# The last steps of a fused attention and feed-forward kernel: alternating PSUM banks, a resting GpSimd, and a last batch stored in halves

## The reference

```python
x = x + attn_a(layernorm(x))   # 16 heads of 64; softmax(q) over features, softmax(k) over tokens,
                               # context = q^T k per head (64x64), then out @ w_out + b_out
x = x + ffn(layernorm(x))      # k_act = relu(xk @ W_k)^2; sigmoid(xr @ W_r) * (k_act @ W_v)
x = x + attn_b(layernorm(x))   # 16 heads of 8 with rotary q and k, full 512x512 softmax, then W_O
x = x + ffn(layernorm(x))      # the same weights again
```

## The kernel before, in words

| step | a | s | l | b | e | us from the span's start |
|---|---|---|---|---|---|---|
| 16 (paired, no A) | - | 15 | 14 | 13 | 12 | about 832 to 885 |
| 17 (draining) | - | - | 15 | 14 | 13 | 885 to 934 |
| 18 (draining) | - | - | - | 15 | 14 | 934 to 972 |
| 19 (draining) | - | - | - | - | 15 | 972 to the end |

## Time and profile before

### The profile page before, as it was taken

How to read it: one execution, slowest core, us unless ns; L and a number is a source line. 1 busy time by engine, 2 the same in 40 slices (tenths; PEclk the granted TensorE clock), 3 DMA queues, 4 the chain that set the end, 5 groups by cost and what they waited for, 6 DMA issues and landing times.

```text
span 1002.2 us, 24337 instructions
## 1 busy us (share of the span) xinstructions
PE 915.6 (91%) x9807; PEld 532.2 (53%) x9807; DVE 651.2 (65%) x1542; ACT 674.6 (67%) x671; POOL 505.9 (50%) x346
## 2 busy tenths in 40 slices
PE   4987989999999999999999999999999998797973
PEld 3775545555555555555555555555555555332322
DVE  4777656668586777668586777668586565635233
ACT  4465677777777777777777777777777777665860
POOL 3758284645566475545566475545566464405000
PEclk9999999999999999999999999999999999998995
DMA  5013243233241423233241423233232323123210
GB/s 165 23 33 103 60 126 90 90 98 115 62 132 52 137 66 98 94 98 115 61 130 54 137 66 101 91 96 116 61 118 57 127 67 121 50 72 99 71 31 16
DMA packets 68669, 87.64 MB, mean 87 GB/s; under 512 B 13633, under 2 KB 40130, under 8 KB 68546
## 3 DMA queue, kind: packets, MB, share of 16 engines
q1 hardware_dynamic: 68546, 85.96, 28.4%
HBM read 16.19 MB, written 20.97 MB: 37 GB/s over the span
## 4 chain that ended last, share of the span: by engine, by line
PE 64%; DVE 14%; ACT 13%; issue 5%; SPq 2%; POOL 1%; DMA 1%; ACTq 0%; DVEq 0%
PE PS L1607 17%; PE PS L1563 9%; PE PS L1407 8%; ACT work L704 6%; PE PS L1409 5%; PE PS L1408 5%; PE PS L1475 5%; PE PS L1521 4%; ACT work_b L704 3%; DVE cT L1099 3%; PE PS L1515 3%; DVE cT L1101 3%; PE PS L1402 2%; PE PS L1504 2%; PE PS L1580 1%
## 5 line engine op out<-in xcount | busy, mean ns | idle before, releaser
L704 ACT ACTIVATE work<-PS 128x2048 f32<-128x2048 f32 x150 | 281.6, 1877 | 53.7 <-PE PS L1563 53.7
L694 ACT ACTIVATE work<-PS 128x512 f32<-128x512 f32 x256 | 152.5, 599 | 175.3 <-PE PS L1409 173.5
L454 POOL TENSOR_TENSOR rs<-ve,half_neg 128x4 f32<-128x4 f32 x64 | 64.8, 1012 | 335.7 <-DVE ve L919 335.7
L1607 PE MATMUL PS<-work,v 128*32 128x512 f32 x1368 | 175.1, 604 | 0.5 <-ACT work L711 0.5
L467 POOL TENSOR_TENSOR work<-work,q_rcp 128x1024 f32<-128x1024 f32 x64 | 122.3, 1911 | 96.4 <-DVE q_rcp L971 59.0
L704 ACT ACTIVATE work_b<-PS 128x2048 f32<-128x2048 f32 x74 | 138.9, 1877 | 24.1 <-PE PS L1563 23.9
L1407 PE MATMUL PS<-wqk,h1h 128*128 128x512 f32 x256 | 124.9, 488 | 5.7 <-issue 2.6
L1563 PE MATMUL PS<-q_st,k_st 32*128 32x512 f32 x896 | 113.8, 496 | 17.6 <-ACT work L704 7.8
L1409 PE MATMUL PS<-wqk,h1l 128*128 128x512 f32 x256 | 101.5, 396 | 0.0
L1408 PE MATMUL PS<-wqk,h1h 128*128 128x512 f32 x256 | 101.2, 395 | 0.0
L1029 DVE SCALAR_TENSOR_TENSOR gated<-gate,PS 128x512 f32<-128x512 f32 x32 | 22.0, 688 | 110.5 <-PE PS L1528 110.5
(11 more groups left out here) (166 smaller groups left out, 1670.6 us busy)
## 6 DMA issues: line engine op xcount, KB each, us to landing
qkv_scratch<-qkv_sb SPq DMA_DIRECT2D x16, 768.0 KB, 4.6
rot<-qkv_sb SPq DMA_DIRECT2D x32, 256.0 KB, 2.4
k_st<-qk_hi SPq DMA_DIRECT2D x128, 64.0 KB, 2.1
q_st<-qk_hi SPq DMA_DIRECT2D x128, 64.0 KB, 2.1
k_st<-qk_lo SPq DMA_DIRECT2D x128, 64.0 KB, 2.1
q_st<-qk_lo SPq DMA_DIRECT2D x128, 64.0 KB, 2.1
parted<-U SPq DMA_DIRECT2D x52, 128.0 KB, 2.9
xa<-in_attn_a_x SPq DMA_DIRECT2D x16, 256.0 KB, 3.3
```

What stands on the lines that cost most here:

```text
L454: pool.tensor_tensor(rs[:, :], ve[:, :], half_neg[:, :], ALU.pow).then_inc(rstd[n].sem, 1)
L694: act.activation((EQ, EK)[r // 2][c % 2][:, (r % 2) * 512:(r % 2) * 512 + 512], PS[:, bank, :], ACT.Exp)\
L704: act.activation(probs_of(z, b, n), PS[:, 0:4, :], ACT.Exp).then_inc(z["s_exp"].sem, 1)
L1607: mm = pe.matmul(PS[32 * h:32 * h + 32, 6, :], v_flat[p][:, kc, at:at + 32], probs_of(z, b, n)[:, h, :], start=(n % 8 == 0), stop=(n % 8 = ...
```

## The change

Steps 0 to 15 are the same instruction for instruction. In step 16, which has no attention A, the products alternate between banks 7 and 4; in the draining steps POOL waits until DVE has finished the layer norm with index 3 (`rest_for_norm`) before it starts on the rotary embedding, and DVE does that norm before `pv_copy`; `mixed_k` is scaled and mixed before `mixed_r` is begun; for the last batch DVE does the square too, `ffn_r` goes to bank 5 and doesn't wait for `relu`, the value product is written to two banks in halves, and the output leaves in two DMAs. `judge_sums` is moved behind the last output. The core of the diff (what is left out are the definitions of three semaphores, the choice of `other`, which is bank 7 with A and 4 without, and the passing of it through `t_copy`, `relu`, `gate_v` and `p_copy`):

```diff
 # SP, draining_step
-                store_out(z, ffn[1], e)
+                if there(b):
+                    store_out(z, ffn[1], e)
+                else:
+                    for half in range(2):
+                        cs = slice(2 * half, 2 * half + 2)
+                        hold(sp, last_x, 0, 2 * half + 2)
+                        sp.dma_start(out_view[e][:, cs, :], out_sb[:, cs, :])\
+                          .then_inc((last_out, z["out_st"])[half].sem, 16)
 # POOL, draining_step
                 rsqrt_var(3, e)
+                rest_for_norm(3, e)
                 if there(l):
...
-                hold(pool, f2["v"], e - 1)
-                square(f2, e)
+                if there(i - 3):
+                    hold(pool, f2["v"], e - 1)
+                    square(f2, e)
 # ACT, paired_step: p_copy(l, 1) only with A; DVE, paired_step, after p_copy(l, 0)
+                    if not A:
+                        p_copy(l, 1, other)
 # ACT, draining_step
-                        gates(f2, e)
+                        gates(f2, e, 4 if there(b) else 5)
 # DVE
+            def mix_k_first(f, j):
+                hold(dve, f["hT"], j)
+                for n in (1, 0):
+                    dve.tensor_scalar(f["mixed"][n][:, :], PS[:, 7, :], mu[:, n:n + 1], None, ALU.mult)\
+                       .then_inc(f["mu"].sem, 1)
+                    hold(dve, f["mu"], j, 2 - n)
+                    dve.scalar_tensor_tensor(f["mixed"][n][:, 1:N], PS[:, 7, 0:N - 1], mu[:, 2 + n:3 + n],
+                                             f["mixed"][n][:, 1:N], ALU.mult, ALU.add).then_inc(f["mix"].sem, 1)
+            def end_half(f, j, half):
+                cs = slice(2 * half, 2 * half + 2)
+                hold(dve, f["gate"], j)
+                hold(dve, last_v, 0, half + 1)
+                dve.scalar_tensor_tensor(gated[:, cs, :], f["gate_sb"][:, cs, :], 1.0, as_chunks(PS[:, (7, 4)[half], :])[:, cs, :],
+                                         ALU.add, ALU.mult).then_inc(last_x.sem, 1)
+                hold(dve, last_x, 0, 2 * half + 1)
+                dve.scalar_tensor_tensor(out_sb[:, cs, :], gated[:, cs, :], 0.5, x3[:, cs, :], ALU.mult, ALU.add)\
+                   .then_inc(last_x.sem, 1)
 # DVE, draining_step
                 x3_stats(z, 3, e)
+                ln_norm(3, e, x3, hn2)
                 if B:
                     pv_copy(z, b, 0)
-                ln_norm(3, e, x3, hn2)
-                scale_and_mix(f2, e)
+                mix_k_first(f2, e)
                 hold(dve, ffn[0]["act"], NB - 1)
-                relu(f2, e)
-                if at_batch(i, NB + 3):
+                if B:
+                    relu(f2, e)
+                else:
+                    relu_sq(f2, e)
+                if B:
+                    gate_v(f2, e) ... add_gated, normalise as before
+                else:
+                    hold(dve, z["out_st"], e - 1)
+                    for half in range(2):
+                        end_half(f2, e, half)
                     judge_sums()
 # PE, paired_step
+                banks, other = ((7,), 7) if A else ((7, 4), 4)
                     if k == 0 and E:
-                        proj_b(l, 1)
+                        if not A:
+                            hold(pe, ph_exp, s)
+                        proj_b(l, 1, banks)
                     if k == 1:
-                        hold(pe, p_ev, l, 3 if E else 1)
-                        ctx_wout(s, spacer=False)
+                        hold(pe, p_ev, l, 1 if not E else 3 if A else 2)
+                        ctx_wout(s, (5, other), spacer=False)
                     if k == 4:
-                        hold(pe, f1["mix"], s)
-                        ffn_k(f1, s, 7)
+                        if A:
+                            hold(pe, f1["mix"], s)
+                        else:
+                            hold(pe, t_ev, s)
+                        ffn_k(f1, s, other)
                     if k == 5:
                         hold(pe, f1["gate"], s)
-                        ffn_v(f1, s)
+                        ffn_v(f1, s, other)
                     if k == 5 and E:
-                        hold(pe, f1["x"], s, 1)
+                        if A:
+                            hold(pe, f1["x"], s, 1)
                         ffn_T(f2, 3, e)
 ... k == 6 and k == 7: ffn_k and ffn_v of f2 to bank `other` in the same way
                     if k == 7:
-                        if E:
+                        if E and A:
                             hold(pe, f2["x"], e, 1)
+                        elif E:
+                            hold(pe, f2["gate"], e)
                         h3_transposes(s)
 # PE, draining_step
                     if n == 12:
-                        ffn_r(f2, e)
+                        if B:
+                            ffn_r(f2, e)
+                        else:
+                            hold(pe, z["x3_ok"], e)
+                            ffn_r(f2, e, "k", 5)
                     if n == 2:
-                        hold(pe, ph_exp, NB - 1)
+                        hold(pe, f2["x"], e - 1, 1)
                     if n == 14:
-                        ffn_v(f2, e)
+                        if B:
+                            ffn_v(f2, e)
+                        else:
+                            last_ffn_v(f2, e)   # chunks 0, 1 to bank 7, then 2, 3 to bank 4, a signal after each pair
```

More of the change, by code:

```diff
@@ L435, in _ @@
                 iterations(filling_step, paired_step, draining_step)
+                hold(sp, last_out, 0)
                 hold(sp, att[0]["out_st"], NB - 1)
@@ L827, in paired_step @@
                 z, f1, f2 = att[0], ffn[0], ffn[1]
+                other = 7 if A else 4
                 for k in range(8):
                     exp_scores(z, b, 2 * k)
-                    if E and k == 1:
+                    if A and E and k == 1:
                         hold(act, qkv_st, l - 1)
@@ L836, in paired_step @@
                     if k == 2:
-                        t_copy(s)
+                        t_copy(s, (5, other))
                     if not E and k == 3:
@@ L1244, in paired_step @@
                 hold(dve, f2["act"], e - 1)
-                relu(f1, s, 7)
+                relu(f1, s, other)
                 if A:
                     sums_of(a, 2)
-                gate_v(f1, s)
+                gate_v(f1, s, other)
                 if E:
@@ L1253, in paired_step @@
                     hold(dve, f1["act"], s)
-                    relu(f2, e, 7)
+                    relu(f2, e, other)
                 ln_norm(2, s, x2, h3)
@@ L1258, in paired_step @@
                 if E:
-                    gate_v(f2, e)
+                    gate_v(f2, e, other)
                     hold(dve, z["out_st"], e - 1)
@@ L1530, in ffn_v, with last_ffn_v @@
                 mm.then_inc(f["v"].sem, 1)
+            def last_ffn_v(f, j):
+                hold(pe, f["act"], j)
+                for c in range(NC):
+                    mm = pe.matmul(PS[:, (7, 4)[c // 2], c * D:(c + 1) * D], f["k_act"][:, c * P:(c + 1) * P], WvfT,
+                                   start=True, stop=True)
+                    if c % 2 == 1:
+                        mm.then_inc(last_v.sem, 1)
             def h3_transposes(j):
@@ L1761, in paired_step @@
                     if k == 4:
-                        hold(pe, f1["mix"], s)
-                        ffn_k(f1, s, 7)
+                        if A:
[3 more added lines that the diff above has]
+                        ffn_k(f1, s, other)
                     if k == 5:
                         hold(pe, f1["gate"], s)
-                        ffn_v(f1, s)
+                        ffn_v(f1, s, other)
                     if k == 6 and E:
-                        hold(pe, f2["mix"], e)
-                        ffn_k(f2, e, 7)
+                        if A:
+                            hold(pe, f2["mix"], e)
+                        else:
+                            hold(pe, f1["x"], s, 1)
+                        ffn_k(f2, e, other)
                     if k == 7 and E:
                         hold(pe, f2["gate"], e)
-                        ffn_v(f2, e)
+                        ffn_v(f2, e, other)
                     if A:
@@ L1855, in draining_step @@
                         hold(pe, f2["mix"], e)
-                        ffn_v(f2, e)
+                        if B:
+                            ffn_v(f2, e)
+                        else:
+                            last_ffn_v(f2, e)
                     if n == 15 and B:
```

18 lines of the change are left out of this document (9 added, 9 removed).

## The result

| | before | after |
|---|---|---|
| median | 1005.38 us (1004.83 to 1007.34, 4 runs) | 994.49 us (992.9 to 995.64, 4 runs) |
| ratio to before, 95% interval | | 0.9887 [0.9869, 0.9905] |
| profiled execution: own time, span | 1004.03, 1002.2 us | 995.63, 993.8 us |

The median is 2.8 us above the forecast of 991.7 and inside its range. A second set of six runs gave 994.44 us (0.9898 [0.9877, 0.9919]). The profiled executions differ by 8.40 us only, because that of before lay 1.35 us under its median and that of after 1.14 us above.

What follows compares the result with a forecast made beforehand. PE bounds the kernel, with its gaps in the last steps. Terms 2.46 + 0.75 + 7.93 - 0.30 + 0.74 + 2.12 + 0.40 = 14.10 us off 1004.03 give 989.93, plus 1.80 for the median: 991.7, range 988.9 to 997.0.

Steps and rivals of the forecast that it cites:

- the norm beside POOL: Step 17: DVE's layer norm no longer waits for POOL; 6.09 us of PE wait plus 1.84 of slow clock, 7.93.
- the stacks before step 18: Batch 15's stack DMAs, now held by POOL, land late for step 18's first tile: 0.30 us lost, bounds 0 and 3.
- the 1 us that the prediction named as a sign of being wrong: The prediction counts as wrong if step 18 starts with a wait over 1 us.
- rival (a): The stacks replace the norm as the wait: PE idles 3 us, the clock drops, time 996.2; chance 0.09.
- Step 18: The norm runs before pv_copy, so PE's wait goes: 0.74 us gained, bounds 0.5 and 0.74.
- step 19: The serial last feed-forward shortens by 2.12 us; 0.45 more if the full clock returns before ffn_v.
- Rival (b): Step 16 is held by the exps and DVE, so the free bank buys nothing: time 994.9; chance 0.07.
- (c): Step 17's norm is slow for a reason other than POOL and still takes 6.45 us: time 996.6; chance 0.02.
- (d): Slower than before: DVE's steady work in step 17 shuts POOL out and stretches the rotary chain; chance 0.03.
- The clock in step 16: A shorter gap and denser PE work may keep the clock full: 0.75 us gained, bounds 0 and 1.25.
- The cover of M: Step 16: DVE ready for M at 849.7, PE at 849.8; if this fails, some tenths are lost.
- the 0.40: Program end: the last DMA, halved to 128 KB, finishes 0.40 us sooner, bounds 0 and 1.4.

Runs made afterwards that it cites:

- no_rest: The changed kernel without POOL's rest before the rotary embedding in the draining steps; 998.42 us, ratio 0.9939 to the kernel before.
- rest_only: The kernel before with only POOL's rest in the draining steps and the layer norm ahead of pv_copy; 1000.1 us, 0.9946.
- keep_busy: verdict_early plus one unused 512-column product into bank 5 before each waiting ffn_r of step 16; 994.64 us, 0.9894.
- no_branch: verdict_early without the conditional second pass that reads the verdict, on all engines; one run, 995.37 us.
- verdict_early: The changed kernel with judge_sums moved from behind the last output into DVE's wait for rsqrt_var in step 19; 993.58 us, 0.9884.
- r_free: verdict_early with step 16's ffn_r waiting only for the key product, not for relu; 990.53 us, 0.9852.
- stacks_first: r_free with SP issuing the stacks ahead of the store of x2 in step 16; 988.22 us, 0.9834.
- no_last_store: verdict_early without the store of the last batch's output; one run, 994.84 us.
- one_store: The changed kernel with the last output in one 256 KB DMA behind the second half; 994.16 us, 0.9891.
- after_again: The changed kernel run again with no edit; 994.44 us over 6 runs.

## Why the prediction was right, and where it was off

**What holds.** Time 991.7 against 994.49, in the range, by the mechanisms named. The largest term, the norm beside POOL, was put at 7.63 net and measured 7.14; no_rest (5.6 us back in step 17) and rest_only (6.95 off) show it by itself. Of the 0.5 missing, 0.22 lies before the transpose of `hn` (one tile took 1.04 us, 0.78 before) and 0.26 behind it. The closest point, the stacks before step 18, cost 0.24 us where I had 0.30; in keep_busy and no_branch the same wait was 1.65 and 1.73, over the 1 us that the prediction named as a sign of being wrong, and step 17 took 43.0 and 43.1 us. So rival (a) does come in part, in some executions. Step 18 (0.79 for 0.74) and step 19 (2.41 for 2.12, the difference being the clock that came back) are right. Rival (b) didn't come (a step 16 of 49.6 us is 3.6 to 3.7 shorter than before's), though the time that it named, 994.9, is nearer to the measured one than the forecast is; no_rest and the norm's 1.12 us refute (c), and POOL's instructions kept their 2.36 us beside DVE, against (d).

**The clock in step 16 was mis-sized.** The step "the gap before the first `ffn_r` of the step, nearly as long, brought no drop" concluded that the first gap is harmless, and the bounds 0 to 1.25 follow from it. In after it is that gap behind which the clock fell. Eight profiles have the new order with both gaps. Three are full (49.71, 49.58, 49.64 us), four with a fall give 52.10 to 52.39, and one has a short fall (no_rest, 50.75). So a fall costs about 2.6 us and came in five of eight; the bound should have reached to -1.4. Without it the banks bring 3.6 to 3.7 us, and the prediction's own terms for a clock that stays give 2.46 + 1.25 = 3.71; with it 1.0. What was wrong is the chance of a fall and its price, not the waits. What the change left in step 16 are the gaps themselves: without them it is 1.5 us shorter than verdict_early's (r_free), and 3.2 with the stacks ahead (stacks_first).

**The cover of M was thin, as said.** `attn_out` waits 0.78 us for `M_sb` at 852.05, where it was 0.38. The copies of q and k did come early, and POOL began on them 3.4 us earlier than before, counted from the start of the step. But SP issued the swap for `rot` only at 841.75, behind its two `parted` issues (840.42 on), and it took half a microsecond longer to land; so `rot` began at 845.25, 0.9 us earlier than before in place of 2.9, and DVE's division ended 0.5 us behind POOL's sum. The queue was the term left out. Some tenths, as the text allowed.

**The end was wrong in sign.** "`judge_sums` (1.3 us) now ends at 995.7, under the DMA, which covers it" failed. I took the landing of the last DMA for what ends the span. It isn't: without that DMA the span still ends 7.4 us behind PE's last matmul (no_last_store). An engine's way out is what is left, with the reading of the verdict and a branch on it (1.4 to 1.7 us of it, no_branch), and the change put the verdict last. That cost 0.9 to 1.1 us (verdict_early), and the 0.40 that halving the store was to bring couldn't come (one_store, no_last_store). The row was there: `out_sb` ended at 996.49 and the DMA took 3.5 us, so it had landed by about 1000.0, 2.2 us ahead of the end of the span. The 0.40 itself had little under it: 256 KB took 3.5 us in before and 2.7 in one_store, and 128 KB took 2.1 in after and 2.7 in no_branch. The split of a DMA's time that the prediction quotes from the Trainium skill (DMA: Bandwidth & Descriptors, "Anatomy of one DMA") is given there for DMAs that GpSimd issues, and SP issues these. For 256 KB it would make 2.6 us, an estimate by that page; the measured times decide.

**The sum.** Median off 10.9 us in place of 14.1. Of the 3.2 missing, the end has 1.8 and step 17 0.5. In step 16 the mean of the eight profiles is 51.1 us, 2.2 off where I had 3.2: 1.0 more, an estimate, since before's 53.32 is one execution too (rest_only had 54.59). Steps 18 and 19 give 0.3 back. That adds up to 3.0. Two terms missed, the clock and the end; that the total stayed inside the stated range is owed to the range's width, not to them.

## What to carry to other kernels

Before costing a change at the end of a program, subtract the last DMA's issue and landing from the span: if time is left over, something else ends it, and a value that every engine reads before leaving belongs early (about 1 us here). A wait that is worth its own length only if the clock holds has two prices, and one profile shows only one of them; look at the same gap in a second execution. When a gap is closed, ask which queue feeds the next tile: here the store ahead of the stacks on SP became the bound at once.

## What the runs showed of the hardware that I had not expected

One program's executions differ in where the clock falls. The gap of 1.88 us before the first `ffn_r` of step 16 was followed by a granted clock of 0.50 in after and of 1.00 in after_again. The same holds for steps 0 to 15, which no kernel changes: from 100 to 110 us the clock was 0.83 in before's profile, 0.50 in after's:

```profile
100.00:110.00 10.00, 8.84 (x90) 5.34 (x94) 7.97 (x27) 5.32 (x5) 4.99 (x5) 0.50 0.27 74
```

and these steps took between 831.31 (one_store) and 838.52 us (rest_only). That may be a good part of the spread of a kernel's runs: in stacks_first they took 836.12 in the profiled execution, its slowest (991.55), while the other four lie between 987.3 and 988.93. The end of the program is drawn in the same way: from the last weighing of step 18 to the last `ffn_k` it was 14.2 us in three profiles of the new step 19, 15.1 in five and 15.6 in two. What decides in which execution the clock falls stays open.

The tail of the stacks varies too. From SP's first issue of batch 15's stacks to the first tile of step 18 it was 6.8 to 7.1 us in after, after_again, verdict_early, one_store, no_last_store and r_free, 7.3 in stacks_first and rest_only, and 8.3 and 8.4 in keep_busy and no_branch, with the same DMAs issued. In the last two a single issue stands out, where most take 0.6 us (keep_busy, then no_branch):

```profile
923.13 1.91 SPq L325 DMA_DIRECT2D q_st<-qk_hi  x1
```

```profile
924.99 1.71 SPq L325 DMA_DIRECT2D q_st<-qk_lo  x1
```

What held these issues up no trace here shows.
